# Splitting the second product of a gated network into three passes, inside a six-layer local-attention kernel

## The reference, cut to what matters

```python
def ffn_layer(x, g, bln, W1, b1, W2, b2):
    mu = x.mean(-1, keepdims=True)
    var = ((x - mu) ** 2).mean(-1, keepdims=True)
    xn = (x - mu) / jnp.sqrt(var + 1e-05) * g + bln
    hg = xn @ W1 + b1
    a, gate = jnp.split(hg, 2, -1)
    return a * jax.nn.gelu(gate, approximate=False) @ W2 + b2
for i in range(6):
    x = attn_layer(shift_tokens(x), Wqkv[i], q_scale[i], k_scale[i], Wo[i]) + x
    x = ffn_layer(shift_tokens(x), ln_g[i], ln_b[i], W1[i], b1[i], W2[i], b2[i]) + x
```

## Time and profile before

| what | value |
|---|---|
| median of 3 runs | 3836.66 us (3831.74 to 3841.37) |
| the profiled execution | 3837.73 us, span of its records 3835.9 us |
| TensorE busy | 3653.4 us, 95% |
| VectorE busy | 3112.8 us, 81% |
| ScalarE busy | 2883.0 us, 75% |
| GpSimd busy | 2569.0 us, 67% |
| granted TensorE clock, mean | 0.98 |

### The profile page before, as it was taken

How to read it: one execution, slowest core, us unless ns; L and a number is a source line. 1 busy time by engine, 2 the same in 40 slices (tenths; PEclk the granted TensorE clock), 3 DMA queues, 4 the chain that set the end, 5 groups by cost and what they waited for, 6 DMA issues and landing times. The chain is left out here.

```text
span 3835.9 us, 189018 instructions
## 1 busy us (share of the span) xinstructions
PE 3653.4 (95%) x70910; PEld 2935.3 (77%) x70910; DVE 3112.8 (81%) x8639; ACT 2883.0 (75%) x8517; POOL 2569.0 (67%) x3324
## 2 busy tenths in 40 slices
PE   7869999999999999999999999999999999899998
PEld 4558888688887788876888868888678887566666
DVE  7878888788887788877888878888788887577766
ACT  5758888478885688875888848888578886577776
POOL 3657877477884787855878747788477884355553
PEclk8979999999999999999999999999999999999999
DMA  1013333233332233332333323333233332100000
GB/s 48 1 54 82 80 82 83 61 82 81 81 81 74 67 82 82 81 88 54 82 82 81 79 64 80 82 81 83 60 82 82 82 80 56 44 1 0 0 1 23
DMA packets 305306, 246.20 MB, mean 64 GB/s; under 512 B 74485, under 2 KB 299860, under 8 KB 304340
## 3 DMA queue, kind: packets, MB, share of 16 engines
q1 hardware_dynamic: 305108, 243.72, 25.2%
HBM read 24.54 MB, written 2.12 MB: 7 GB/s over the span
## 5 line engine op out<-in xcount | busy, mean ns | idle before, releaser
L1252 POOL TENSOR_TENSOR wa_t<-wa_t 128x256 f32<-128x256 f32 x1536 | 1092.9, 733 | 342.9 <-DVE wa_t L1045 342.6
L903 ACT ACTIVATE wa_pb<-wa_sc,wa_nm 128x64 f32<-128x64 f32 x3072 | 670.1, 329 | 361.6 <-DVE wa_nm L1090 337.7
L1242 POOL TENSOR_TENSOR wa_t<-wa_t,wa_rn 128x512 f32<-128x512 f32 x768 | 785.3, 1043 | 227.5 <-DVE wa_rn L1068 224.7
L1044 DVE TENSOR_TENSOR wa_t<-wa_pj,wa_ctab 128x512 f32<-128x512 f32 x768 | 528.4, 688 | 206.1 <-PE wa_ta L645 160.6
L45 PE MATMUL wa_pj<-lw_wqkv_high,wa_xhigh 128*128 128x512 f32 x1152 | 530.9, 461 | 35.3 <-DVE wa_t L1045 16.2
L886 ACT ACTIVATE wa_sq<-wa_pj 128x512 f32<-128x512 f32 x768 | 485.7, 634 | 67.0 <-PE wa_pj L47 65.4
L1045 DVE TENSOR_TENSOR wa_t<-wa_pj,wa_stab 128x512 f32<-128x512 f32 x768 | 523.0, 681 | 0.0
L47 PE MATMUL wa_pj<-lw_wqkv_high,wa_xlow 128*128 128x512 f32 x1152 | 460.6, 400 | 0.0
L46 PE MATMUL wa_pj<-lw_wqkv_low,wa_xhigh 128*128 128x512 f32 x1152 | 457.4, 397 | 0.0
L1050 DVE TENSOR_REDUCE wa_raw<-wa_sq 128x16 f32<-128x1024 f32 x384 | 449.2, 1170 | 0.0
L704 PE MATMUL wa_ob<-wa_oT,lw_wo 128*128 128x128 f32 x3120 | 419.8, 278 | 2.3 <-DVE wa_on L1102 2.3
(11 more groups left out here) (308 smaller groups left out, 8208.5 us busy)
## 6 DMA issues: line engine op xcount, KB each, us to landing
wa_vv<-wa_vt SPq DMA_DIRECT2D x2304, 65.0 KB
wa_vv<-wa_vt SPq DMA_DIRECT2D x1152, 32.5 KB
lw_wqkv<-L_ffn_Wqkv SPq DMA_DIRECT2D x6, 1536.0 KB, 6.1
lw_xs<-yT SPq DMA_DIRECT2D x96, 64.0 KB
lw_fs<-yT SPq DMA_DIRECT2D x48, 128.0 KB
lw_xs<-yT SPq DMA_DIRECT2D x96, 63.8 KB
lw_fs<-yT SPq DMA_DIRECT2D x96, 63.8 KB
lw_wo<-L_ffn_Wo SPq DMA_DIRECT2D x6, 512.0 KB, 4.2
```

The source lines that it names most:

```text
L903: last = nc.scalar.activation(pb[:, u.par(2), p, e, :], SC[:, e, p * KEYS:(p + 1) * KEYS], ACT.Exp, bias=nm[:, u.par(2), e, p:p + 1])
L1044: nc.vector.tensor_tensor(t1[:, b, j], x, table(ctab), ALU.mult)
L1242: nc.gpsimd.tensor_tensor(here, here, rn[:, u.par(1), j * HG:(j + 1) * HG].unsqueeze(2).broadcast_to((128, HG, HD)), ALU.mult).then_inc(s. ...
L1252: last = nc.gpsimd.tensor_tensor(here, here, t2[:, b, j, :, of], ALU.add)
```

## The change

W2 is split into a high and a low part, as W1 already was, and so is the gated product. Each down product becomes three passes of short-form matmuls. Per group and chunk this adds `hidden_high` on ScalarE (a copy with rounding of `gm_hid`) and `hidden_low` on GpSimd (`gm_hid` minus the high part). `gm_hid` shrinks from three to two buffers used in turn, so `gated` now waits for the `hidden_low` of two chunks earlier instead of for the down product; `down` waits for `hidden_low`, and `hidden_high` waits for the down product of the same chunk one group earlier. Each down product stands one place later on TensorE. On VectorE `close(u-1)` moves behind `gated` 1. On GpSimd `turn` moves from the first place of a group to the last. The rounding copy of `split_weights` moves from GpSimd to ScalarE (`weights_high`). The split of W2 is four GpSimd instructions for each layer, in the first two slots of the layer's last full sequence. The new lists of `multiply(u)`:

W2's loads count on a semaphore of their own. Two constant tables used only at the start, and the buffers of the first input, are given back before the layers' tiles are placed; no instruction is added by that. The diff, cut to its core:

```diff
@@ layer_weights @@
-        w2=sb("w2", [128, GCH, D]), b1=sb("b1", [128, 2, GCH]),
+        w2=sb("w2", [128, GCH, D]), w2p=[sb("w2_" + n, [128, GCH, D], F32R) for n in parts], b1=sb("b1", [128, 2, GCH]),
@@ weight_columns @@
+def weight_columns(u):
+    return slice((u.at - 1) * WCOLS, u.at * WCOLS) if u.loop is None else bass.ds(
+        u.loop * (2 * WCOLS) + (u.at - 1) * WCOLS, WCOLS)
@@ local_layers @@
-        hid = gb("hid", [128, GCH, GRP])
+        hid = gb("hid", [128, 2, GRP])
+        high, low = ([gb(f"hid_{n}{j}", [128, GRP], F32R) for j in range(GCH)] for n in ("high", "low"))
@@ TensorE @@
                 def down(u, j):
                     r = glu_rows(j)
-                    pe.wait_ge(s.act_done, u.n(GCH, j + 1))
+                    pe.wait_ge(s.low_done, u.n(GCH, j + 1))
                     if j == 0 and u.at > 0:
                         pe.wait_ge(s.y_out, u.n(1, 1))
-                    last = nc.tensor.matmul(Y[:, :], w2[0:r, j, :], hid[0:r, j, :],
-                                            start=(j == 0), stop=(j == GCH - 1))
-                    if j == GCH - 1:
-                        last.then_inc(s.down_done, 1)
+                    three_passes(nc, Y[:, :], [x[0:r, j, :] for x in w2p], [x[j][0:r, :] for x in (high, low)],
+                                 start=(j == 0), stop=(j == GCH - 1)).then_inc(s.down_done, 1)
                 def multiply(u, turn_later, norm_next, split_next):
                     pe.wait_ge(s.xn_parts, u.n(1, 1))
                     chunk(u, 0)
-                    down(u.before(), 2)
+                    down(u.before(), 1)
                     chunk(u, 1)
                     norm_next()
-                    down(u, 0)
+                    down(u.before(), 2)
                     turn_later()
                     chunk(u, 2)
-                    down(u, 1)
+                    down(u, 0)
                 def closing(u, one, two):
                     pe.wait_ge(s.xn_parts, u.n(1, 1))
                     chunk(u, 0)
-                    down(u.before(), 2)
+                    down(u.before(), 1)
                     keys_queries(one)
                     chunk(u, 1)
-                    down(u, 0)
+                    down(u.before(), 2)
                     values(one)
                     chunk(u, 2)
                     keys_queries(two)
+                    down(u, 0)
                     down(u, 1)
                     down(u, 2)
                     values(two)
...
                     chunk(first, 1)
                     norm(LayerGroup(layer, 1))
                     slot(Slot(layer, 4, NB))
-                    down(first, 0)
                     turn(LayerGroup(layer, 2))
                     chunk(first, 2)
-                    down(first, 1)
+                    pe.wait_ge(s.w2_low, 2 * layer + 2)
+                    down(first, 0)
                     groups(pe, layer, multiply, closing, turn, norm)
                     if final:
+                        down(LayerGroup(layer, NGRP - 1), 1)
                         down(LayerGroup(layer, NGRP - 1), 2)
                 slot(Slot(0, 0, 0))
@@ ScalarE @@
                     nc.scalar.activation(gl[0:r, j % 2, :], GT[j % 2][0:r, :], ACT.Gelu,
                                          bias=b1[0:r, 1, j:j + 1]).then_inc(s.gelu_done, 1)
+                def hidden_high(u, j):
+                    r = glu_rows(j)
+                    act.wait_ge(s.act_done, u.n(GCH, j + 1))
+                    if u.has(1):
+                        act.wait_ge(s.down_done, u.n(GCH, j + 1, 1))
+                    nc.scalar.activation(high[j][0:r, :], hid[0:r, (u.par + j) % 2, :], ACT.Copy).then_inc(s.high_done, 1)
+
+                def weights_high(u):
+                    act.wait_ge(s.proj_done, u.layer * (3 * UPL) + 3 * UPL)
+                    act.wait_ge(s.w_loaded, u.layer * 48 + 96)
+                    here = weight_columns(u)
+                    full, hi = (x[:, :, :].rearrange("p t n -> p (t n)") for x in (lw.wqkv_full, wqkv[0]))
+                    nc.scalar.activation(hi[:, here], full[:, here], ACT.Copy).then_inc(s.w_high, 1)
+
                 def multiply(u, turn_later, norm_next, split_next):
                     gelu(u, 0)
+                    if 1 <= u.at <= NGRP - 2 and not u.final:
+                        weights_high(u)
+                    hidden_high(u, 0)
                     gelu(u, 1)
                     norm_next()
                     split_next()
+                    hidden_high(u, 1)
                     gelu(u, 2)
+                    hidden_high(u, 2)
                 def closing(u, one, two):
                     gelu(u, 0)
                     squares(one, 0)
                     squares(one, 1)
+                    hidden_high(u, 0)
                     gelu(u, 1)
+                    hidden_high(u, 1)
                     values(one)
                     gelu(u, 2)
+                    hidden_high(u, 2)
                     nc.scalar.preload_act_table_set("natural_log_exp_and_others")
                     slot(two)
...
+                    split(LayerGroup(layer, 1))
+                    hidden_high(first, 0)
+                    hidden_high(first, 1)
                     gelu(first, 2)
-                    split(LayerGroup(layer, 1))
+                    hidden_high(first, 2)
                     groups(act, layer, multiply, closing, None, norm, split)
                 slot(Slot(0, 0, 0))
@@ VectorE @@
                     dve.wait_ge(s.a_done, u.n(GCH, j + 1))
-                    if j < 2:
-                        wait_chunk(dve, s.down_done, u, 1, 0)
+                    if j == 2 or u.at > 0:
+                        dve.wait_ge(s.low_done, u.n(GCH, j - 1))
                     nc.vector.scalar_tensor_tensor(
-                        out=hid[0:r, j, :], in0=AT[j % 2][0:r, :], scalar=b1[0:r, 0, j:j + 1],
+                        out=hid[0:r, (u.par + j) % 2, :], in0=AT[j % 2][0:r, :], scalar=b1[0:r, 0, j:j + 1],
                         in1=gl[0:r, j % 2, :], op0=ALU.add, op1=ALU.mult).then_inc(s.act_done, 1)
                 def close(u):
-                    dve.wait_ge(s.down_done, u.n(1, 1))
+                    dve.wait_ge(s.down_done, u.n(GCH, GCH))
                     nc.vector.scalar_tensor_tensor(out=yT[:, u.cols()], in0=Y[:, :], scalar=vec[:, 2:3],
                                                    in1=yT[:, u.cols()], op0=ALU.add, op1=ALU.add).then_inc(s.y_out, 1)
                 def multiply(u, turn_later, norm_next, split_next):
                     norm_next()
-                    close(u.before())
                     gated(u, 0)
                     gated(u, 1)
+                    close(u.before())
                     turn_later()
                     split_next()
                     gated(u, 2)
...
                         make_tables(u.layer + 2)
                 def closing(u, one, two):
-                    close(u.before())
                     gated(u, 0)
                     rotate(one, 0)
                     rotate(one, 1)
                     gated(u, 1)
+                    close(u.before())
                     sums(one)
                     clamp(one)
                     gated(u, 2)
@@ GpSimd @@
                         pool.wait_ge(s.w1_loaded, u.layer * 16 + 16)
                         nc.gpsimd.tensor_tensor(w1[0][:, :], lw.w1_full[:, :], g.zero.broadcast_to((128, 2 * GLU)),
                                                 ALU.add).then_inc(s.w1_high, 1)
+                    if u.lead == NB - 1 and u.k < 2:
+                        rows, part = (GW, slice(0, GCH - 1)) if u.k == 0 else (glu_rows(GCH - 1), slice(GCH - 1, GCH))
+                        pool.wait_ge(s.w2_loaded, u.layer * 32 + 32)
+                        nc.gpsimd.tensor_tensor(w2p[0][0:rows, part, :], w2[0:rows, part, :], g.zero[0:rows].unsqueeze(2).broadcast_to(
+                            (rows, part.stop - part.start, D)), ALU.add).then_inc(s.w2_high, 1)
+                        pool.wait_ge(s.w2_high, 2 * u.layer + u.k + 1)
+                        nc.gpsimd.tensor_tensor(w2p[1][0:rows, part, :], w2[0:rows, part, :], w2p[0][0:rows, part, :].bitcast(F32),
+                                                ALU.subtract).then_inc(s.w2_low, 1)
...
                 def split_weights(u):
-                    here = slice((u.at - 1) * WCOLS, u.at * WCOLS) if u.loop is None else bass.ds(
-                        u.loop * (2 * WCOLS) + (u.at - 1) * WCOLS, WCOLS)
-                    pool.wait_ge(s.proj_done, u.layer * (3 * UPL) + 3 * UPL)
-                    pool.wait_ge(s.w_loaded, u.layer * 48 + 96)
-                    nc.gpsimd.tensor_tensor(hi[:, here], full[:, here], g.zero.broadcast_to((128, WCOLS)),
...
+                def hidden_low(u, j):
+                    r = glu_rows(j)
+                    pool.wait_ge(s.high_done, u.n(GCH, j + 1))
+                    nc.gpsimd.tensor_tensor(low[j][0:r, :], hid[0:r, (u.par + j) % 2, :], high[j][0:r, :].bitcast(F32),
```

(15 more changed lines are left out.)

24 lines of the change are left out of this document (13 added, 11 removed).

## The result

The changed kernel takes 3876.34 us (median of four runs, 3873.07 to 3877.16). The kernel before took 3838.05 in runs on the same chip. The ratio is 1.0102, with a 95% interval of 1.0090 to 1.0114: slower by 1%. The forecast was 3874 us, 1.0% slower. The profiled execution took 3876.22 us with a span of 3874.4, against 3837.73 and 3835.9 before, so 38.5 us are to be found.

What follows compares the result with a forecast made beforehand. TensorE bounded the kernel before; a ring through four engines, 8.7 us a group, would bound the gated network. Five layers at +6.4 (32.0) and the last at +5.5 gave +37.5 us: 3874.2 us, range 3853 to 3900.

Steps and rivals of the forecast that it cites:

- TensorE's own account: TensorE's matmuls in a gated-network group: three passes save 0.17 us a product, 0.51 a group, 7.80 to 7.29.
- up to group 0's `gated 0` (W2's split): Attention slots: W2's split on GpSimd makes TensorE wait for normalise, 0.3 us a layer, bounds 0 and 1.0.
- `gated 0` to `norm(3)`: Start of the gated network: 13.6 us instead of 14.2, 0.6 gained.
- `norm(3)` to `norm(7)`: Four groups of the gated network at 8.7 us: 34.8 against 31.05, 3.75 lost.
- `norm(7)` to the first projection: End of the gated network to the next layer: 8.65 us against 8.1, 0.55 lost.
- first projection to `values(two)`: In closing: three more ScalarE copies make values(two) start 2.4 us later than before.
- pause after the jump: TensorE's 3.29 us pause after its jump back in closing moves along and hides nothing.
- a layer with `closing`: Sum for each of five layers: 3.15 + 0.55 + 2.4 + 0.3 = 6.4 us lost, 32.0 in all.
- last layer, `norm(7)` to `close`: Last layer's end: the last close starts 16.75 us after norm(7) instead of 14.7, 2.0 lost.
- The circle: Gated-network groups: a wait chain through VectorE, ScalarE and GpSimd makes a group 8.7 us, bounds 8.36 and 9.05.
- The overlap: GpSimd's low 1 runs alongside VectorE's split (gm_xlow) in each group and is stretched by 0.33 us.
- The clock: Rival: waits drop TensorE to half clock in a third of the 36 groups, 70 us more, 3945 us; chance 0.08.

Runs made afterwards that it cites:

- e8: Changed kernel with all four W2 split instructions in the third slot of the layer's second sequence, not the last sequence's first two; 3877.6 us, ratio 1.0108.
- e9: Changed kernel with turn, gelu 1, the weights' subtraction and split_input moved earlier, down products and close(u-1) later; 3831.7 us, ratio 1.0004 to the kernel before.
- e4: Kernel before, old order, with each down product as three passes of rounded operands, low parts left out; 3819.2 us, ratio 0.9956.
- e7: Changed kernel with split_input ahead of the previous group's low 2 on GpSimd in closing; 3866.5 us, ratio 1.0080.
- e2: Changed kernel with gelu 1 ahead of high 0 on ScalarE; 3880.6 us, ratio 1.0118.
- e1: Changed kernel with turn ahead of low 1 on GpSimd; 3880.3 us, ratio 1.0119.

## Why the prediction was right, point by point

The mechanism was right: one chain through four engines, longer than TensorE's own account, sets the pace of a group. The total was right too, but that it came within 1 us of the measured one is luck: the terms below are off by up to 1.2 us a layer in both directions, and they made up for one another. First layer, in us, each term the shift against the kernel before:

| step | forecast | measured |
|---|---|---|
| up to group 0's `gated 0` (W2's split) | +0.3 | +1.52, of it 0.7 to 1.1 the split, the rest mostly clock |
| `gated 0` to `norm(3)` | -0.6 | -0.35 (13.83 for 14.18) |
| `norm(3)` to `norm(7)` | +3.75 | +2.51 (33.56 for 31.05) |
| `norm(7)` to the first projection | +0.55 | +1.54 (9.65 for 8.11) |
| first projection to `values(two)` | +2.4 | +2.36 (12.17 for 9.81) |
| pause after the jump | 0 | -0.18 (4.08 for 4.26) |
| a layer with `closing` | +6.4 | +7.40, all five 7.19 on average |
| last layer, `norm(7)` to `close` | +2.0 | +0.93 (15.64 for 14.71) |
| behind the last `close` | 0 | -2.07 |
| the whole | +37.5 | +38.5 |

The average of 7.19 comes from `norm(7)`: 3.68 late in the first layer, 39.64 in the last, and five layers between. Where the 2.07 us behind the last `close` went was not followed. W2's split, sized at 0.3 with 1.0 as its upper bound, is the term that was farthest off for its size: e8 shows that GpSimd's room covers less of it than I took.

- **TensorE's own account.** Right: 0.23 between passes, and with the waits gone (e9) a group takes 7.3, forecast 7.29. With the old order (e4) it was 7.45, where short waits are left.
- **The circle.** Its links are there in the order forecast, 8.39 for 8.7, at the low end of the forecast's 8.4 to 9.1. But with `high 1` sooner than forecast, the release of `low 1` was shared: I had the weights' subtraction done at 5.5, just ahead of `low 1` at 5.75, and it was done at 5.39 and let `low 1` go at that time. Its ScalarE part was sized too long: I gave every copy its full 0.64 plus a gap. The rows show that a copy is followed after 0.54 (`high 0` 723.77, `gelu 1` 724.31). From `norm` to `high 1` it was 4.62 us where I had 5.04 (5.68 less its own 0.64). That a group of instructions follows itself faster than its duration stood in the old trace too, on VectorE: `gm_xlow` of 0.66 at 741.21, the next at 741.78.
- **The overlap.** Half right. It was there in every group and cost the circle about what I gave it, but in another place: `low 1` was first and took its usual 1.28, and VectorE's `gm_xlow` (L1174), which came second, took 1.13. GpSimd's first `turn` instruction then met what was left of `gm_xlow` and took 0.64, not 0.20. I had 0.33 on `low 1`; it was 0.44 on `turn`.
- **norm(7) to the first projection.** This step failed. I followed ScalarE's chain and counted GpSimd's list as covered; but `split_input`, which the projection waits for, is queued behind `low(6, 2)`. e7 takes 1.46 us off it.
- **closing.** Right to 0.04 us. The chain was as written: `high 1` at 5.49 after the first projection (forecast 5.5), `high 2` at 8.26 (8.35), the table at 8.90 (9.0).
- **The last layer.** Sized too dear by 1.1. Group 7's `gated 0` ended 8.52 after `norm(7)` (forecast 9.4), and the last `close` started 7.1 behind that (7.35): the first part again held copies and a `chunk` that came sooner, as the circle was shorter.
- **The clock.** The rival that TensorE would fall to its lower level in the waits, in a third of the groups, did not come. At 1.1 us of waiting in 8.4 the granted clock of the stage was 1.00 in four of the six layers. But in the third and fourth layer it was 0.96, with matmuls 0.43 apart instead of 0.23 for some 3 us in group 1, where the kernel before stays at 1.00. The turn in question took 11.17 and 11.18 us instead of 9.65. These are two single turns, 3 us of the 38.5, for which the sum had nothing. Stage of the third layer in the changed kernel:

```profile
1729.60:1772.90 43.30, 38.52 (x176) 28.89 (x175) 31.31 (x89) 26.54 (x44) 33.26 (x31) 0.96 0.12 28
```

- **What it missed.** That the circle did not stand alone: the way through `low 0` and the weights' subtraction is as long, and the one over TensorE and VectorE that e2's last layer shows is 0.1 to 0.2 us shorter. The total did not need it, but the remedy did: each edit that the prediction's own circle pointed to (e1, e2) gained nothing by itself.

The contention rule of the Trainium skill that the prediction drew on (GPSIMD Engine Reference, section 8, Key points) holds here, with the sides told by the rows: of two that overlapped, the one that began second was stretched, VectorE's two-input subtraction from 0.66 to 1.2, and GpSimd's small addition behind it from 0.20 to 0.64.

## What to carry to other kernels

Work that fits on idle engines still costs if it goes into the chain that leads from one group to the next. Follow that chain through every engine's list, one turn round, and compare its length, not the busy shares, with the bounding engine's own account. When a cut of the longest circle brings nothing, look for the next one of the same length, and for one that the cut itself has closed, before giving the theory up: here two moves that each cut the first circle brought nothing alone, and with four more they took the group from 8.4 to 7.3. And a step that is put ahead of another in a queue delays whatever waits for that other one, in this kernel the next layer's first projection.
